# Vision tower on one core: logits taken from turned values instead of through a fused weight, the first pair loaded in longer rows, all sequences set anew

## What is computed

```python
h  = patches @ W.T + b                              # 1024 x 256
v  = h @ w1.T + b1                                  # "values", 256
w  = softmax((v @ ww.T + bw).reshape(.., 16, 31))   # 16 heads, 31 taps ("logits", 496)
acc = sum_k w[..., k:k+1] * shifted(v, k)           # along the image axis, 16 long
attn = layer_norm(h + acc @ w2.T + b2) * gamma + beta
h  = layer_norm(h + attn)
# FFN with quantised activations (absmax to 127 steps) and ternary weights:
# down( silu(gate(h)) * up(h) ), inner width 1024
out = layer_norm(h + ffn(h))
```

## Time and profile before

| | us |
|---|---|
| median of 3 runs | 121.08 (120.03 to 121.67) |
| the profiled execution, whole | 120.99 |
| its span, first to last instruction | 119.2 |
| TensorE's steady run starts (first `embed(1,0)`) | 17.3 |
| last matmul ends | 111.4 |

### The profile page before, as it was taken

How to read it: one execution, slowest core, us unless ns; L and a number is a source line. 1 busy time by engine, 2 the same in 40 slices (tenths; PEclk the granted TensorE clock), 3 DMA queues, 4 the chain that set the end, 5 groups by cost and what they waited for, 6 DMA issues and landing times.

```text
span 119.2 us, 2371 instructions
## 1 busy us (share of the span) xinstructions
PE 104.6 (88%) x716; PEld 66.7 (56%) x716; DVE 79.2 (66%) x187; ACT 69.2 (58%) x124; POOL 79.3 (67%) x147
## 2 busy tenths in 40 slices
PE   6949999999999999999999999999999988775300
PEld 2538367768756475676746756666665754443200
DVE  5301974445646575577978997887978899788510
ACT  0042019826293036359536997887688799788520
POOL 6995000020259799998997488788888889888830
PEclk9999999999999999999999999999999999999955
DMA  3999999962223231220132130224310000010231
GB/s 98 348 308 354 432 392 425 403 256 35 24 58 37 55 31 43 25 28 1 50 28 32 39 32 6 58 27 99 35 32 29 0 0 0 3 43 19 69 89 53
DMA packets 22532, 12.20 MB, mean 102 GB/s; under 512 B 18036, under 2 KB 20596, under 8 KB 22135
## 3 DMA queue, kind: packets, MB, share of 16 engines
q1 hardware_dynamic: 21436, 10.39, 31.0%
q10 hardware_dynamic: 1082, 1.65, 4.2%
HBM read 9.70 MB, written 2.34 MB: 101 GB/s over the span
## 4 chain that ended last, share of the span: by engine, by line
PE 61%; POOL 16%; DMA 8%; issue 6%; DVE 3%; ACTq 1%; POOLq 1%; DVEq 0%
PE bank L356 13%; PE bank L431 11%; PE bank L414 11%; PE bank L397 6%; PE bank L458 5%; DMA bias_row<-in_bias 4%; POOL q L1118 4%; DMA xT<-in_xT 3%; PE bank L489 3%; PE bank L505 3%; POOL f L1125 3%; POOL rstd L1032 2%; PE bank L544 2%; PE bank L412 2%; PE bank L444 1%
## 5 line engine op out<-in xcount | busy, mean ns | idle before, releaser
L1083 POOL TENSOR_TENSOR taps<-probs,inv_total 128x256 f32<-128x256 f32 x8 | 5.1, 636 | 22.2 <-DVE inv_total L792 22.1
L356 PE MATMUL bank<-xT,tokW 128*128 128x256 f32 x72 | 16.6, 380 | 0.0
L431 PE MATMUL bank<-conv_w,vpad 128*32 128x128 f32 x256 | 15.8, 399 | 0.0
L356 PEld LDWEIGHTS bank<-xT,tokW 128*128 128x128 f32 x72 | 13.6, 190 | 3.5 <-issue 1.8
L414 PE MATMUL bank<-wl,h1T 128*128 128x496 f32 x32 | 14.6, 578 | 0.0
L431 PEld LDWEIGHTS bank<-conv_w,vpad 128*32 128x32 f32 x256 | 8.2, 122 | 6.1 <-issue 2.5
L666 ACT ACTIVATE gu<-bank,sc 128x512 f32<-128x512 f32 x16 | 11.0, 685 | 1.2 <-PE bank L489 1.1
L854 DVE TENSOR_TENSOR gu<-gu,bank 128x512 f32<-128x512 f32 x16 | 10.9, 681 | 1.0 <-ACT gu L666 0.8
L1118 POOL TENSOR_SCALAR q<-gu,sc 128x512 f16<-128x512 f32 x14 | 9.9, 708 | 1.3
L771 DVE TENSOR_REDUCE top<-bank 128x16 f32<-128x496 f32 x8 | 5.4, 672 | 8.0 <-PE bank L414 8.0
L544 PE MATMUL bank<-w_q,q2T 128*128 128x256 f16 x64 | 8.4, 272 | 2.4 <-ACT q2T L680 2.0
(11 more groups left out here) (120 smaller groups left out, 231.5 us busy)
## 6 DMA issues: line engine op xcount, KB each, us to landing
xT<-in_xT SPq DMA_DIRECT2D x3, 768.0 KB, 13.7
w_raw<-in_wg SPq DMA_DIRECT2D x1, 1024.0 KB, 10.7
w_raw<-in_wu SPq DMA_DIRECT2D x1, 1024.0 KB, 12.7
w_raw<-in_wd SPq DMA_DIRECT2D x1, 1024.0 KB, 15.6
shear<-taps SPq DMA_DIRECT2D x8, 128.0 KB, 1.7
conv_w<-shear SPq DMA_DIRECT2D x64, 16.0 KB, 1.9
out_dram<-res SPq DMA_DIRECT2D x7, 128.0 KB
ww<-in_ww SPq DMA_DIRECT2D x1, 496.0 KB, 5.7
```

What stands on the lines that cost most here:

```text
L356: last = nc.tensor.matmul(ps_embed(pair, m), tokW[:, k, m * P:(m + 1) * P], xT[:, pair, k, :], start=(k == 0), stop=(k == KC_PATCH - 1))
L431: last = nc.tensor.matmul(ps_yT[j * SLOT:(j + 1) * SLOT, k, :], vpad[:, s, h, :], conv_w[:, s, :, h], start=(par == 0), stop=(par == 1))
```

## The change

The fused weight `wl` and all that made it go. Instead `values_turned(pair, m)` makes half of a pair's values with features on partitions (`w1` stationary, the pair's `h1T` moving, 256 columns, two products), and ACT puts them into `vT` with the bias b1 (`out_vT`). `logits(t)` takes `vT` and `ww` as they are. `values(t)` becomes two f32 transposes of `vT`, as in `residual`. The turned values use banks 5 and 0, shared with `inner_transposes`, `down` and `embed`, with the waits for that. The first pair's `tokW` and `xT` stand in one array `first`, 2 KB per partition and k, loaded in four parts of k (1, 1, 2, 2), partitions 0 to 63 by SP, 64 to 127 by ACT. The waits for `tokW_in[1]` and `x0_in[1]` go, `ww` moves to ACT's queue, `w1o` goes. The bias row is shorter by 256. The last tile's scale gets a semaphore of its own, and `spread(7)` is issued ahead of `store(0)`. The sequences of TensorE, ACT, DVE and POOL are written anew; the start of each is shown.

```diff
-FIRST = [0, 1, 3]
+FIRST = [0, 1, 2, 4]
...
+        first = sb("first", [P, KC_PATCH, D + 2 * P])
+        xT = sb("xT", [P, PAIRS - 1, KC_PATCH, 2 * P])
+        tokW, xT_first = first[:, :, 0:D], first[:, :, D:D + 2 * P]
...
+        vT = sb("vT", [P, TILES, KC, P])
...
+        ps_vT = [bank[5][:, 0:2 * P], bank[0][:, 0:2 * P]]
...
-                sp.dma_start(tokW[:, k0:k1, :], tokW_d[:, k0:k1, :]).then_inc(tokW_in[i], 16)
-            sp.wait_ge(tokW_in[1], 16)
-            sp.dma_start(ww[:], ww_d).then_inc(ww_in, 16)
+                sp.dma_start(first[0:P // 2, k0:k1, :], first_d[0:P // 2, k0:k1, :]).then_inc(first_in[i], 16)
             sp.dma_start(w1[:], w1_d).then_inc(w1_in, 16)
-            sp.dma_start(xT[:, 1], xT_d[1]).then_inc(x_in[1], 16)
+            sp.dma_start(xT[:, 0], xT_d[0]).then_inc(x_in[1], 16)
             sp.dma_start(w_raw[:, 0], wg_d).then_inc(ffn_in[0], 16)
             sp.dma_start(w_raw[:, 1], wu_d).then_inc(ffn_in[1], 16)
-            sp.dma_start(xT[:, 2], xT_d[2]).then_inc(x_in[2], 16)
+            sp.dma_start(xT[:, 1], xT_d[1]).then_inc(x_in[2], 16)
...
-            put_taps(4); spread(4); put_taps(5); spread(5); put_taps(6); spread(6); put_taps(7); store(0)
-            spread(7); store(1); store(2); store(3); store(4); store(5); store(6); store_half(sp, 0)
+            put_taps(4); spread(4); put_taps(5); spread(5); put_taps(6); spread(6); put_taps(7); spread(7)
+            store(0); store(1); store(2); store(3); store(4); store(5); store(6); store_half(sp, 0)
...
+                        pe.wait_ge(first_in[FIRST.index(k)], 32)
...
-            def logit_bias():
-
-                pe.wait_ge(b1_ww_ok, 1)
-                nc.tensor.matmul(ps_bw, ones[:], b1_ww[:], start=True, stop=True).then_inc(bw_ps, 1)
-
-            def logit_weights():
-
-                pe.wait_ge(ww_in, 16)
-                pe.wait_ge(w1o_in, 16)
-                for m in range(KC):
-                    for k in range(KC):
-                        last = nc.tensor.matmul(ps_wl[m], w1o[:, k, m * P:(m + 1) * P], ww[:, k, :],
-                                                start=(k == 0), stop=(k == KC - 1))
-                    last.then_inc(wl_ps, 1)
+            def values_turned(pair, m):
+
+                pe.wait_ge(w1_in, 16)
+                pe.wait_ge(h1T_ok, 2 * pair + 2)
+                if m == 0:
+                    if put["vT5"]:
+                        pe.wait_ge(vT_ok, put["vT5"])
+                    if put["turned"]:
+                        pe.wait_ge(q2T_ok, put["turned"])
+                    put["vT5"] = 2 * pair + 1
+                else:
+                    pe.wait_ge(h1T_ok, put["embed0"])
+                    if put["down"]:
+                        pe.wait_ge(down_read, put["down"])
+                    if put["vT0"]:
+                        pe.wait_ge(vT_ok, put["vT0"])
+                    put["vT0"] = 2 * pair + 2
+                for k in range(KC):
+                    last = nc.tensor.matmul(ps_vT[m].rearrange("p (t n) -> p t n", t=2), w1[:, k, m * P:(m + 1) * P],
+                                            h1T[:, 2 * pair:2 * pair + 2, k, :], start=(k == 0), stop=(k == KC - 1))
+                last.then_inc(vT_ps, 1)
...
-                if j0 == 0:
-                    pe.wait_ge(bias_ok, 2)
-                else:
+                if j0 > 0:
...
-                nc.tensor.matmul(ps_v, bias_pick[0:65], bias_mm[0:65, LOGITS:LOGITS + D], start=True, stop=False)
                 for k in range(KC):
-                    last = nc.tensor.matmul(ps_v, h1T[:, t, k, :], w1[:, k, :], start=False, stop=(k == KC - 1))
+                    last = nc.tensor.matmul(ps_v[:, k * P:(k + 1) * P], vT[:, t, k, :], ident[:], is_transpose=True,
+                                            start=(k == 0), stop=True, skip_group_check=True)
...
-                    last = nc.tensor.matmul(ps_logits, h1T[:, t, k, :], wl[:, k, :], start=False, stop=(k == KC - 1))
+                    last = nc.tensor.matmul(ps_logits, vT[:, t, k, :], ww[:, k, :], start=False, stop=(k == KC - 1))
...
+                if half == 0:
+                    pe.wait_ge(vT_ok, put["vT5"])
+                    if t > 0:
+                        pe.wait_ge(q2T_ok, t)
+                    put["turned"] = t + 1
...
                     pe.wait_ge(h1T_ok, put["embed0"])
+                    pe.wait_ge(vT_ok, put["vT0"])
...
+            first_embeds(); embed(1, 0); values_turned(0, 0); embed(1, 1); values_turned(0, 1); residual(0)
+            values_turned(1, 0); values(0); embed(2, 0); logits(0); weight_means(0, 2); embed(2, 1); logits(1)
+            values_turned(1, 1); weight_means(2, 3); values_turned(2, 0); values(1); values_turned(2, 1)
+            logits(2); embed(3, 0); logits(3); conv(0); logits(4); project_out(0); conv(1); values(2)
+            residual(1); embed(3, 1); project_out(1); logits(5); residual(2); conv(2); values_turned(3, 0)
+            in_transposes(0); project_out(2); values(3); gate(0, 0); up(0, 0); values_turned(3, 1); up(0, 1)
+            gate(0, 1); conv(3); residual(3); logits(6); in_transposes(1); project_out(3); gate(1, 0); up(1, 0)
...
-            def out_wl():
-                act.wait_ge(wl_ps, 1)
-                nc.scalar.copy(wl[:, 0, :], ps_wl[0]).then_inc(wl_act_ok, 1)
+            def out_vT(pair, m):
+
+                act.wait_ge(vT_ps, 2 * pair + m + 1)
+                nc.scalar.activation(vT[:, 2 * pair:2 * pair + 2, m, :], ps_vT[m].rearrange("p (t n) -> p t n", t=2),
+                                     ACT.Identity, bias=b1[:, m:m + 1]).then_inc(vT_ok, 1)
...
-                act.dma_start(xT[:, 0, k0:k1], xT_d[0, :, k0:k1]).then_inc(x0_in[i], 16)
+                act.dma_start(first[P // 2:P, k0:k1, :], first_d[P // 2:P, k0:k1, :]).then_inc(first_in[i], 16)
             act.dma_start(bias_cols[:], cols_d).then_inc(cols_in, 16)
-            act.wait_ge(x0_in[1], 16)
-            act.dma_start(w1o[:], w1o_d).then_inc(w1o_in, 16)
             act.wait_ge(bias_zero_ok, 1)
             for j in range(3):
                 act.dma_start(bias_row[32 * j:32 * j + 1, :], bias_d).then_inc(bias_in, 16)
+            act.dma_start(ww[:], ww_d).then_inc(ww_in, 16)
             act.dma_start(w2[:], w2_d).then_inc(w2_in, 16)
...
+            out_h1T(0, 0); out_h1T(0, 1); out_h1T(1, 0); out_vT(0, 0); out_h1T(1, 1); out_vT(0, 1)
+            weight_sum(0); out_v(0); weight_sum(1); out_h1T(2, 0); weight_sum(2); exps(0); out_h1T(2, 1)
+            out_vT(1, 0); weight_round(1); out_vT(1, 1); out_v(1); exps(1); out_vT(2, 0); out_vT(2, 1); exps(2)
+            negate_gamma(); out_h1(0); out_h1T(3, 0); out_yT(0); exps(3); weight_finish(1); out_h1(1); exps(4)
+            out_v(2); out_yT(1); centre(0); out_h1T(3, 1); out_h1(2); quant_in(0); exps(5); out_yT(2); centre(1)
...
-            def bias_product():
-
-                dve.wait_ge(cols_in, 16)
-                dve.wait_ge(ww_in, 16)
-                after(mark(nc.vector.tensor_scalar(b1_ww[:], ww[:, 0, :], b1[:, 0:1], None, ALU.mult)))
-                nc.vector.scalar_tensor_tensor(b1_ww[:], ww[:, 1, :], b1[:, 1:2], b1_ww[:], ALU.mult,
-                                               ALU.add).then_inc(b1_ww_ok, 1)
-
-            def logit_bias_rows():
-
-                dve.wait_ge(bw_ps, 1)
-                after(mark(nc.vector.tensor_tensor(bias_row[0:65, 0:LOGITS], bias_row[0:65, 0:LOGITS], ps_bw[0:65],
-                                                   ALU.add)))
-                bias_rows(0, LOGITS)
...
+            bias_rows(0, LOGITS); bias_rows(LOGITS, BIASES); top_logits(0); shift(0); weight_scales(0, 2)
+            tap_sums(0); tap_inverses(0); top_logits(1); shift(1); weight_scales(2, 3); tap_sums(1)
...
+            normalise(0); weight_round(0); normalise(1); normalise(2); weight_clip(1); weight_clip(0)
+            weight_round(2); add_beta(0); inv_std_attn(0); weight_clip(2); inv_std_mid(0); normalise(3)
+            normalise(4); add_beta(1); inv_std_attn(1); weight_finish(0, wq_gate_ok); add_beta(2)
+            inv_std_mid(1); out_scales(0); scale_h3(0); inv_std_attn(2); out_scales(1); inner_limit(0)
+            inner_limit(1); normalise(5); inv_std_mid(2); scale_h3(1); add_beta(3); quant_inner(0, 0)
+            inv_std_attn(3); quant_inner(0, 1); weight_finish(2, wq_down_ok); inv_std_mid(3); normalise(6)
+            scale_h3(2); out_scales(2); add_beta(4); out_scales(3); inner_limit(2); add_h3(0); normalise(7)
...
```

210 lines of the change are left out of this document (85 added, 125 removed).

## The result

| | before | after |
|---|---|---|
| median of 4 runs each | 121.38 (120.03 to 121.76) | 122.23 (121.85 to 123.56) |
| the profiled execution | 120.99 | 121.92 |
| its span | 119.2 | 120.1 |
| first `embed(1,0)` | 17.27 | 13.15 |
| `inv_std_attn(3)` on POOL begins | 64.94 | 66.60 |

The ratio after to before on record is 1.0125, with a 95% interval of 1.0071 to 1.0180; it is an estimate from the single runs and not the quotient of the two medians, which is 1.0070. That is less than the 2% a single comparison can tell, but the interval leaves 1 out: the change costs about 1%. I had forecast 120.0 us, 0.9% faster. The time lies in the range of 117.2 to 123.0; the sign is wrong.

The account below looks back on a forecast made before the run. TensorE early and POOL from 35 us were taken as the bounds: normalise(2) at 38.6, plus 73.5 work and 1.3 waits, gives 113.4; 4.8 behind it and 1.8 around the span give 120.0 us, range 117.2 to 123.0.

Parts of the forecast that it names:

- The landing of the first pair: Loads before the steady run: 355 GB/s, near the middle earlier flow row; `embed(1,0)` starts at 12.5 us, 4.8 earlier.
- The bounds of 11.0 and 14.7: Limits in us for the second pair's landing: 427 GB/s throughout with a 1.5 us tail, or as before.
- The point that sets the end: POOL behind normalise(2): from 38.6 us, 73.5 us of work and 1.3 of waits, ending at 113.4.
- that costs: TensorE up to `logits(2)`: starts 4.8 us earlier but does 8.6 us more, so normalise(2) ends at 38.6.
- The other engines at nothing: ACT's added evacuations, DVE's 2.5 us less bias work and the added `vT_ok` waits were costed at nothing.
- TensorE's work: Whole kernel: 12.0 us removed, 8.8 added, sum -3.3 us, all of it ahead of 17.3 us.
- TensorE's lead in the second half: TensorE, 3 us ahead there, was to take away most of POOL's 4.0 us of waits.
- B: Rival: TensorE's gain gets through, second pair lands by 11.2 us and POOL never waits; 117.9 us, chance 0.18.
- C: Rival: TensorE's clock falls in the 2.8 us hole before the steady run, 1.7 us lost; 121.7 us, chance 0.22.
- D: Rival: second pair lands no earlier than before, 14.7 us; 123.9 us, over 2% slower from about 14.3; chance 0.12.
- E: Rival: the longer load rows bring nothing and the orders level out; 121.1 us, chance 0.06.
- A: Likeliest case: POOL bounds the kernel to the end, as summed; 120.0 us, own range 118.7 to 121.5, chance 0.42.

Follow-up runs that it names:

- load_by_k: Changed kernel with each part of the first pair in one transfer over all 128 partitions, parts alternating between SP and ACT; 121.69 us, ratio 1.0064 to before.
- by_k_warm: load_by_k with nine warm-up products instead of six and the second pair's transfer ahead of `w1`; 120.42 us, ratio 0.9976 to before.
- logits2_ahead: by_k_warm with both `values_turned(2,·)` behind `logits(2)` on TensorE and `exps(2)` ahead of `out_vT(2,·)` on ACT; 123.29 us, ratio 1.0200 to before.
- pool_early: Changed kernel with POOL's clips, `weight_finish(2)` and `quant_inner(0,1)` moved earlier into its holes; 122.69 us, ratio 1.0131 to before.
- stats_first: by_k_warm with DVE's `attn_stats(3)` and `attn_variance(3)` ahead of `top_logits(6)` and `shift(6)`; 121.89 us, ratio 1.0101 to before.
- turned_old_order: Changed kernel with all four engines in the sequences of the kernel before, turned values put in pair by pair; 127.11 us, ratio 1.0490 to before.
- te_late_more: Changed kernel with conv(5)'s 32 products done twice, 1.9 us more on TensorE; 123.89 us, ratio 1.0233 to before.
- before_halves: Kernel before with only the new loading: halves of 64 partitions, no waits between the loads; 123.68 us, ratio 1.0223 to before.
- second_pair_late: by_k_warm with the gate weight ahead of the second pair's transfer, making a hole ahead of `embed(1,0)`; 125.44 us, ratio 1.0370 to before.
- te_early_less: Changed kernel with one product left out of each `values_turned` of the first three pairs (values wrong); 122.58 us, ratio 1.0125 to before.

## Why the prediction was wrong

**The landing of the first pair.** Forecast: 355 GB/s, first embeds done at 9.7, second pair at 12.5. Measured: 258 to 267 GB/s, first embeds done at 12.4, second pair at 13.1 (issued at 3.9, 9.2 to landing), start 13.15. The step took the rows of 2 and 4 KB as better than those of 1 KB and chose "near the middle row"; it did not ask what the cut into halves of 64 partitions does. load_by_k has the same rows at full height and gets 401 to 413. In size this is 0.65 us of the sum, since the late first embeds only ate most of the hole (0.57 instead of 2.8 us). The bounds of 11.0 and 14.7 held it. The step also left out a wait: `embed(1,0)` needs a bank that ACT first empties of the first embeds (the trace names `out_h1T` as what ended the hole). Here both came at the same moment; in load_by_k and by_k_warm the bank alone set the start.

**The point that sets the end.** Forecast: normalise(2) ends at 38.6, then 73.5 us of work and 1.3 of waits. Measured: 39.75, 73.0 and 2.8. The step itself is wrong and not just its terms: logits2_ahead has normalise(2) earlier and the end later, and pool_early takes 2.6 us from behind `inv_std_attn(3)` and gains nothing. What holds is the difference of 48.9 to 49.1 us from `inv_std_attn(3)` to POOL's end, in seven kernels of the changed structure in which nothing between the two was moved, with starts from 11.3 to 14.5 us. From `inv_std_attn(4)` it is 39.8 to 39.9 us in the same seven and in pool_early and stats_first too, where the difference from `inv_std_attn(3)` is 48.6 and 50.7. So the end hangs on when POOL gets to `inv_std_attn(4)`; in the changed kernel the last thing it waits for on the way is `inv_std_attn(3)`, and that wait ends on TensorE. The prediction had this place in hand: it walked to `project_out(3)` at 63.9 and booked the wait of 1.2 us as a remainder, when the sum had to run over it.

**The sum over the right path.** Forecast: start 12.5, `project_out(3)` at 63.9, `inv_std_attn(3)` at 64.7, POOL's end at 113.4, so 51.4, 0.8 and 48.7 us between them. Measured: 13.15, 65.47, 66.60, 115.55, so 52.3, 1.1 and 48.95. Late by 0.65 (landing), 0.9 (TensorE), 0.33 (`attn_stats(3)` stood behind `shift(6)` on DVE) and 0.25: 2.15 us. Behind POOL's end 4.55 us were left instead of 4.8, so the profiled execution is 1.9 us above the forecast, and the median 2.2. Of TensorE's 0.9, 0.4 stands ahead of `logits(2)`, which ended 22.7 us after the start (34.16 + 1.67 net) instead of 22.3.

**The change against the kernel before**, on the same path: the start is 4.1 us earlier, but TensorE needs 52.3 us from there to the end of `project_out(3)` instead of 46.7, then DVE 1.1 instead of 0.9, then POOL 48.95 instead of 49.46. -4.1 + 5.6 + 0.2 - 0.5 = +1.2 us. Of the 5.6, 4.7 are eight halves of turned values less what `values(1)` to `values(3)` no longer take (7.0 - 3 x (0.98 - 0.22)), 0.4 are `residual(0)` and `values(0)`, which stood ahead of the start before, and -0.2 is `inner_transposes(0,0)`, which the new order puts behind `project_out(3)`. The 0.7 left are groups that each took a little longer, and no run looks into them. The prediction had said that the step "that costs" was the work ahead of `logits(2)`; the account runs on to `project_out(3)`.

**The other engines at nothing.** Right for the bias work on DVE, whose saving was larger than costed and gave the end nothing, and for the added waits; ACT's `out_vT` is no wait in the new sequences and is one in turned_old_order and logits2_ahead. **TensorE's work.** The rows it was costed from hold (0.87, 0.22, 1.88); TensorE's lead in the second half was overrated (0.8 us at conv(5), by te_late_more).

**Rivals.** B did not come: the lead was not there. C did not, since the hole closed; its mechanism is real and its price higher. D did not: 13.1 against its 14.3. E's 121.1 is nearer in number than A's, but the orders did not level out. A was the one that came in its mechanism at the end (POOL bound, no wait behind 67 us) with its terms 2.15 us too good.

What stays open: why the clock's column reads 1.00 from 3 to 9 us while the first embeds run at half rate (below), and why the executions of the changed kernel differ there. pool_early, whose loads are the same, ran them at full rate with holes between and started at the same 13.2 us, so the end of the changed kernel did not depend on it; that of load_by_k did. What sets POOL's arrival at `inv_std_attn(4)` in pool_early, engine by engine, was not followed up.

## What to carry to other kernels

Look for the point behind which all experiments would keep the same distance to the end, and sum every engine's path *up to it*; here it lay in the middle of the schedule, just behind a wait that ended on TensorE, and was not the first result that the last engine needs. A distance that stays the same while nothing behind the point is moved shows little: move work across the point and see whether it still holds. An earlier start is worth only what is not put back as work between it and this point, and filler work on TensorE that covers an evacuation can't be moved away for free. Two structures are compared only when both are loaded and warmed up alike: here that took the new one from about 1% slower to level, and the old one, given the same, gained as well.

## What the runs showed of the hardware

- A load cut into two transfers of 64 partitions each, on two queues, moved 249 to 267 GB/s from 3 to 9 us (after, before_halves), and 213 to 280 in the five other traces loaded so; the same bytes with the same row lengths in half as many whole-height transfers moved 401 to 414 (load_by_k, by_k_warm), and 374 to 421 in the seven other traces loaded so. The kernel before, at full height with shorter rows and its waits between the loads, had 346 and 306.
- A DVE instruction with two SBUF inputs (`attn_norm`) stood still beside a POOL pass of 1.9 us: 1.78 instead of 0.48 us in stats_first, and 1.24 us at 54.67 in the changed kernel, beside `weight_finish(0)` from 53.73 to 55.63. The Trainium skill, "GPSIMD Engine Reference", section "1. Specifications", says that POOL's access to SBUF is shared with VectorE and contends with instructions of this kind; the traces agree, with 1.3 us as the price in stats_first.
- The first embeds ran at 0.43 us per instruction until about 10 us in the changed kernel (7 instructions in 3.00 us) and at 0.22 in by_k_warm for most of them (15 in 3.00 us), both with a granted clock of 1.00 in the column. Nine warm-up products ahead of them went with the faster rate in all eight traces that have them. Six went with the slower one in six traces of eight with the new array (before_halves and pool_early are the others), and with the faster one in the kernel before. No run here says what makes the difference.
- Behind a hole of 3.19 us the granted clock was 0.50 and cost 2.5 us of the end (second_pair_late); behind holes of 1.1 and 1.5 us (pool_early, te_early_less) 12 instructions took 2.86 us, full rate.
